# Thirty-two small experts in one stage: second-layer weights held in two column halves, hidden activations streamed

## The reference, cut to what matters

```python
def _L2_ffn_ref(x, router_w, router_b, W1, b1, W2, b2):
    xf = x.reshape(-1, D)                      # D = 64
    logits = xf @ router_w.T + router_b
    idx = jnp.argmax(logits, axis=-1)          # one of 32 experts
    h = jnp.einsum('nd,ndh->nh', xf, jnp.take(W1, idx, axis=0)) + jnp.take(b1, idx, axis=0)
    h = jax.nn.relu(h)                         # 16 hidden units
    out = jnp.einsum('nh,nhd->nd', h, jnp.take(W2, idx, axis=0)) + jnp.take(b2, idx, axis=0)
    return jax.nn.relu(out).reshape(x.shape)
...
h = h + _L2_ffn_ref(_layernorm(h, axis=-1), ...)
```

## Time and profile before

| | us |
|---|---|
| median of 3 runs | 5232.56 |
| lowest and highest | 5227.27, 5240.82 |
| the profiled execution | 5234.82 |
| its span | 5233.0 |
| PE busy | 4141.6 (79%) |
| DVE busy | 2849.0 (54%) |
| ACT busy | 2239.6 (43%) |
| mean granted clock of PE | 0.859 |

### The profile page before, as it was taken

One profiled execution on the slowest core, in us unless ns is written; L12 is line 12 of the kernel. 1 busy time (PEld: TensorE's weight loads), 2 busy tenths in 40 slices (PEclk: granted clock), 3 DMA queues, 4 the chain that ended last, 5 costly groups with the idle time before them and its releaser, 6 DMA issues. The chain is left out here.

```text
span 5233.0 us, 70744 instructions
## 1 busy us (share of the span) xinstructions
PE 4141.6 (79%) x26824; PEld 2791.7 (53%) x26824; DVE 2849.0 (54%) x6188; ACT 2239.6 (43%) x3791; POOL 494.8 (9%) x824
## 2 busy tenths in 40 slices
PE   6785865899887865899887864799887875799887
PEld 4664644565555634465555633555546554555646
DVE  4555746355545746355545747355554747355555
ACT  3342665254241656254242655144432448144432
POOL 0100000201100010201100010111100110111100
PEclk9898976799888986799888886699998986699998
DMA  2000000000000000000000000000000000000000
GB/s 86 3 3 16 1 17 1 0 1 1 1 1 4 1 17 1 0 1 1 1 1 4 1 17 1 0 1 1 1 1 4 1 1 1 1 1 1 1 1 4
DMA packets 28313, 26.52 MB, mean 5 GB/s; under 512 B 10550, under 2 KB 26934, under 8 KB 27450
## 3 DMA queue, kind: packets, MB, share of 16 engines
q1 hardware_dynamic: 27962, 21.98, 1.5%
HBM read 20.40 MB, written 1.57 MB: 4 GB/s over the span
## 5 line engine op out<-in xcount | busy, mean ns | idle before, releaser
L719 ACT ACTIVATE big<-ps,negmax 128x1024 f32<-128x1024 f32 (+1 forms) x672 | 600.1, 899 | 262.3 <-DVE negmax L752 262.2
L752 DVE TENSOR_REDUCE negmax<-ps 128x1 f32<-128x1536 f32 x336 | 590.0, 1758 | 39.3 <-PE ps L622 19.8
L705 ACT COPY big<-ps 128x512 f32<-128x512 f32 x672 | 394.1, 586 | 494.4 <-PE ps L646 491.4
L646 PE MATMUL ps<-cst,big 128*128 128x128 f32 x4032 | 503.3, 275 | 30.3 <-ACT big L719 29.8
L646 PEld LDWEIGHTS ps<-cst,big 128*128 128x128 f32 x4032 | 457.9, 142 | 48.3 <-ACT big L719 39.7
L436 ACT COPY xt<-ps 64x512 f32<-64x512 f32 x144 | 78.5, 580 | 817.5 <-PE ps L428 817.5
L423 PE MATMUL ps<-cst 128*128 128x512 f32 x608 | 319.0, 682 | 127.8 <-DVEq L190 58.2
L615 PE MATMUL ps<-kup,qup 128*128 128x512 f32 (+3 forms) x768 | 357.0, 562 | 41.9 <-POOLq L190 41.1
L408 POOL TENSOR_TENSOR st<-st,cst 128x6 f32<-128x6 f32 x104 | 156.9, 1508 | 2306.9 <-DVE st L396 2302.8
L662 PE MATMUL ps<-big,v 128*32 128x128 f32 (+1 forms) x8064 | 321.9, 277 | 8.1 <-DVE ctxt L1197 6.0
L615 PE MATMUL ps<-klo,qlo 128*128 128x512 f32 (+3 forms) x672 | 313.7, 550 | 2.2
(11 more groups left out here) (397 smaller groups left out, 7451.4 us busy)
## 6 DMA issues: line engine op xcount, KB each, us to landing
rw<-in_w_route SPq DMA_DIRECT2D x128, 64.5 KB, 1.9
cst<-in_consts SPq DMA_DIRECT2D x1, 2671.0 KB, 14.9
cst<-in_consts SPq DMA_DIRECT2D x1, 2670.5 KB, 9.0
big<-in_consts SPq DMA_DIRECT2D x1, 1872.5 KB, 22.2
out_dram<-res SPq DMA_DIRECT2D x4, 384.0 KB, 2.8
experts_in<-in_consts SPq DMA_DIRECT2D x1, 1360.0 KB, 17.7
qup<-in_patches SPq DMA_DIRECT2D x4, 260.0 KB
klo<-in_pe_low SPq DMA_DIRECT2D x2, 384.0 KB, 23.5
```

The lines of the kernel that those rows point to most:

```text
L646: ins = nc.tensor.transpose(turned_bank(kind, u, g)[:, i * P:(i + 1) * P], prob[:, slot_of(kind, u), (4 * g + i) * P:(4 * g + i + 1) * P], ...
L705: copy(pt[:, slot_of(kind, u), g, 0:n], turned_bank(kind, u, g)[:, 0:n]).then_inc(*ph.mark(copier(kind, g)))
L719: nc.scalar.activation(prob[:, slot_of(kind, u), cols], src[:, cols], ACT.Exp, bias=bias, accum_out=part_sum[:, u, k:k + 1]).then_inc(*ph. ...
L752: nc.vector.tensor_reduce(negmax[:, u:u + 1], flat[:, 0:n], AX.X, ALU.max, negate=True)\
```

## The change

The 12 x 5 = 60 products of the second layer become 15 products with 512 moving columns and 12 that join two halves. For each block of 512 tokens (`outputs`), `w2_2` is stationary in four chunks of 128x64, and `hid` moves. Chunks 0 and 2 go into partitions 0 to 63 of a bank, chunks 1 and 3 into partitions 64 to 127; the bias is added into the lower half by a product with K = 32. ACT copies the bank (128x512) to `both_halves`, a part of the buffer `qup` (`add_halves`). Then four products for each block (`added`) hold 128x128 of `both_halves` stationary and move `fold[64]`, into banks 6 and 7, which DVE reads in place of 4 and 5. The first layer's products keep their number and shape, but are written in three blocks with the second layer's between them.

```diff
+                def add_halves(j):
+                    act.wait_ge(*ph.after("halves_psum", j + 1))
+                    nc.scalar.copy(both_halves[:, 512 * j:512 * (j + 1)], ps[:, 4 + j % 2, :]).then_inc(*ph.mark("halves_copied"))
...
+                    if j == NB - 1 and c in (1, 3):
+                        add_halves(c // 2)
+                add_halves(2)
...
-                pe.wait_ge(*ph.after("hid_ready", NB * C2))
-                for t in range(T):
-                    o = ps[:, 4 + t // 6, (t % 6) * D:(t % 6 + 1) * D]
-                        nc.tensor.matmul(o, hid[:, c, t * P:(t + 1) * P], K("w2_2")[:, c * D:(c + 1) * D], start=(c == 0), stop=False)
-                    ins = nc.tensor.matmul(o, xt2[64:96, t * P:(t + 1) * P], K("b2_2")[64:96, :], start=False, stop=True)
...
+                def outputs(j):
+
+                    pe.wait_ge(*ph.after("hid_ready", (j + 1) * C2))
+                    if j > 1:
+                        pe.wait_ge(*ph.after("halves_copied", j - 1))
+                    for c in range(C2):
+                        strip = ps[D * (c % 2):D * (c % 2) + D, 4 + j % 2, :]
+                        nc.tensor.matmul(strip, K("w2_2")[:, c * D:(c + 1) * D], hid[:, c, 512 * j:512 * (j + 1)],
+                                         start=(c < 2), stop=(c == C2 - 1), skip_group_check=True)
+                    nc.tensor.matmul(ps[0:D, 4 + j % 2, :], K("b2_2")[64:96, :], xt2[64:96, 512 * j:512 * (j + 1)],
+                                     start=False, stop=True, skip_group_check=True).then_inc(*ph.mark("halves_psum"))
+
+                def added(j):
+
+                    pe.wait_ge(*ph.after("halves_copied", j + 1))
+                    for t in range(4 * j, 4 * j + 4):
+                        ins = nc.tensor.matmul(ps[:, 6 + t // 6, (t % 6) * D:(t % 6 + 1) * D], both_halves[:, t * P:(t + 1) * P],
+                                               fold[D][:, :], start=True, stop=True)
...
+                hidden(0)
+                hidden(1)
+                outputs(0)
+                hidden(2)
+                outputs(1)
+                added(0)
+                outputs(2)
+                added(1)
+                added(2)
```

More of the change, by code:

```diff
@@ L75 @@
     "moe2": {"rstd_ready": 2, "xt_copied": 6, "hid_ready": 12, "xt_psum": 6, "logit_psum": 1, "hid_psum": 12,
-        "out_psum": 2, "vec_step": 18, "var_ready": 2, "normed": 2},
+        "out_psum": 2, "halves_psum": 3, "halves_copied": 3, "vec_step": 18, "var_ready": 2, "normed": 2},
     "rel3a": {"pool_step": 8, "upper_cleared": 1, "rstd_ready": 4, "rot_used": 6, "xt_copied": 3, "qv_ready": 6,
@@ L286, in build @@
         sparse = work
+        both_halves = qup[:, 1, :]
         qt = qlo[:, 0, :]
@@ L1609, in _ @@
                 transpose_pe(ph, xa, [4, 5, 6], width=P)
[L1610 to L1617, removed]
@@ L1618, in _, with hidden @@
-                pe.wait_ge(*ph.after("hid_ready", NB * C2))
-                for t in range(T):
-                    o = ps[:, 4 + t // 6, (t % 6) * D:(t % 6 + 1) * D]
-                    for c in range(C2):
-                        nc.tensor.matmul(o, hid[:, c, t * P:(t + 1) * P], K("w2_2")[:, c * D:(c + 1) * D], start=(c == 0), stop=False)
-                    ins = nc.tensor.matmul(o, xt2[64:96, t * P:(t + 1) * P], K("b2_2")[64:96, :], start=False, stop=True)
-                    if t % 6 == 5:
-                        ins.then_inc(*ph.mark("out_psum"))
+                def hidden(j):
+                    pe.wait_ge(*ph.after("xt_copied", NB + j + 1))
+                    for c in range(C2):
+                        if j > 0:
+                            pe.wait_ge(*ph.after("hid_ready", (j - 1) * C2 + c + 1))
+                        nc.tensor.matmul(ps[:, c, :], K("w1_2")[:, c * P:(c + 1) * P], xt2[:, 512 * j:512 * (j + 1)],
+                                         start=True, stop=True).then_inc(*ph.mark("hid_psum"))
@@ new lines, in added @@
+                def added(j):
[3 more added lines that the diff above has]
+                                               fold[D][:, :], start=True, stop=True)
+                        if t % 6 == 5:
+                            ins.then_inc(*ph.mark("out_psum"))
+                hidden(0)
@@ L1939, in _ @@
                     dve.wait_ge(*ph.after("out_psum", i + 1))
-                    nc.vector.scalar_tensor_tensor(h[:, 6 * i:6 * i + 6, :], rows_bank([4, 5], i), 0.0, h[:, 6 * i:6 * i + 6, :],
+                    nc.vector.scalar_tensor_tensor(h[:, 6 * i:6 * i + 6, :], rows_bank([6, 7], i), 0.0, h[:, 6 * i:6 * i + 6, :],
                                                    ALU.max, ALU.add)
```

## The result

The changed kernel takes 5183.8 us (median of 4 runs, 5177.4 to 5190.1) where the kernel before took 5236.7 (5227.3 to 5243.5): a ratio of 0.990, 95% interval 0.9878 to 0.9922. That is 52.9 us less; 60 were forecast (5172, range 5155 to 5203). The profiled executions are 5234.8 and 5177.4, 57.4 apart. Run again beside the experiments, it took 5175.7 against 5235.1 (0.9892, 0.9875 to 0.9908): 59.4 us less.

A forecast was written before the change was run, and what follows sets the result against it. PE's time in moe2 was taken as the bound: 11.9 us an image in place of 28.2 saves 65 us, with 5 given back, so 5174.8 profiled and 5172.5 for the median; range 5155 to 5203.

The forecast's parts named there:

- What bounds the stage: In moe2 PE works last, so its time there is on the path one to one; 112.7 us to be replaced.
- The halves pair: New second layer: two column halves run side by side, eight 512-column records in 1.8 us.
- Bias and joining: New second layer: bias 1.2 us a block with shape changes; joinings 2.7 us an image, plus 0.2 for the tail.
- First layer: moe2's 12 first-layer products stay; image 1's first 3.45 us run at the lower level, 12.2 us before and after.
- the 65 us: moe2's second layer: 11.9 us an image at the upper level in place of 28.2, 65 us saved in all.
- Waits: moe2: ACT's copies are covered, at most 0.2 us; without cover about 0.9; the old 0.69 us wait goes.
- The clock in the new layer: moe2's second layer keeps the upper level, being dense; the old had a wide load before each short record.
- Rival 1: The clock falls in moe2's new layer as in the old: 30 us given back, 5203; chance 0.14 whole or in part.
- What is given back in rel3a: Longer PE idle time before L428 can bring the slower pattern, up to 13.6 us either way; 4 us taken.
- Rival 3: Weight loads stay in the open between the new layer's strips: 3.6 us in all, 5176, or 5180; chance 0.06.
- rival 4: Halves don't pair and the clock falls in moe2's new layer: 17 us more, 5250; chance 0.02.

The follow-up runs named there:

- experiment 2: Changed kernel without the two column halves, all four chunks summed in the lower 64 partitions: 5191.5 us, ratio 0.9918 to the kernel before.
- experiment 7: Changed kernel with each block's joining directly behind its own outputs, so PE waits for ACT's copy: 5187.3 us against 5231.8 for the kernel before.
- experiment 3: Kernel before with one 512-column filler product behind each of the 12 tiles of moe2's second layer: 5234.9 us against 5235.1.
- experiment 4: Kernel before with a 512-column filler behind every second tile of moe2's second layer, six an image: 5204.7 us, ratio 0.9937.
- experiment 5: Changed kernel with 24 filler products in place of 15 at the start of rel3a: 5155.5 us, ratio 0.9853 to the kernel before.
- experiment 6: Kernel before with 21 filler products in place of 15 at the start of rel3a: 5223.8 us against 5231.8, ratio 0.9990.
- experiment 9: Changed kernel with 24 rel3a fillers, bias cut into both halves, nine moe2 fillers for four and four new behind the logits: 5145.2 us against 5231.8.
- experiment 10: Changed kernel with 24 rel3a fillers and the bias cut into both halves, moe2's fillers untouched: 5148.8 us against 5235.1, ratio 0.9835.
- experiment 11: Changed kernel with 24 rel3a fillers, cut bias, eight moe2 fillers for four and two new behind the logits: 5138.7 us against 5235.1, ratio 0.9818.

## Why the prediction was right, point by point

- **What bounds the stage.** Right. PE's time in moe2 was on the path one to one: 65.4 us less there. Against the forecast for the profiled execution (5174.8, measured 5177.4) 6 us more were lost behind the stage than the 5 taken (11.0, all in rel3a), and 3.4 were gained in stages that the change doesn't touch. That the two nearly cancel is luck.
- **The halves pair.** Right, and shown by taking the pairing away (experiment 2): 1.87 us for eight records against 3.58. The row of attn2 with 128 columns and that of attn4 with 512 bounded it well.
- **Bias and joining.** The bias was priced at 1.2 us and took 1.0; the joinings with the tail at 2.9 and took 1.03 + 2.00 = 3.0. Second layer and joinings together take 22.28 - 10.65 = 11.6 us at the upper level, 11.9 were given.
- **First layer.** That its slow start "is so before and after" in image 1 was wrong: the level rose with its first product there, and 3.2 to 3.5 us late in images 2 and 4 instead. Over four images it takes 46.2 us, before 45.7, so the sum didn't suffer.
- **What the 65 us are made of**, which the prediction doesn't say. An estimate from the earlier trace rows and these measurements: at the upper level the old layer would take 16.7 us, so of the 28.2 an image 10.8 are the lower level and 0.7 the wait, and the new layer's 11.6 saves another 5.1 by its products. Over four images that is 43 for the clock, 3 for the wait and 20 for the products; experiment 2 puts the pairing at 21.7.
- **Waits.** Right: none in the stage. With the cover gone (experiment 7) a wait costs 0.74 us where 0.9 was given, and in two images of four the level fell as well.
- **The clock in the new layer.** Right. Of the reason given, that in the old layer a wide load stands before each short record, half is shown: dense records among the short ones keep the upper level (experiments 3 and 4). That it is the load and not the shortness is not shown. Rival 1 did not come; its neighbour with three idle gaps an image lost the level in two images, beside idle time.
- **What is given back in rel3a.** The place was right: the level behind PE's idle time, as experiment 5 shows by filling that time. I took 4 us, and it is 11 in the first profile; all four images showed the slow pattern, in both profiles. The end of the range for this (13.6) was nearly reached. With 11 in place of 4 the forecast would have been about 5180, between the two medians measured. The step that failed is the reason given, that a longer idle time brings the slow pattern. The kernel before already spoke against it: its fast images idle 6.17 us, and image 3, a slow one, idles less:

```profile
3386.76 2.77 PE L428 MATMUL ps<-cst,x 128*64 128x128 f32 x12 [5.79 <-DVE st L418]
```

Behind 8.1 us of idle time 18 profiled images are slow and 5 fast (experiments 3 and 4), and behind 5.1 to 6.5 us 6 are slow and 3 fast (the kernel before, experiments 2 and 7). What chooses between the two patterns stays open. Only with the idle time cut to 1.1 us or less (experiments 5, 6, 9, 10 and 11) was L442 or L441 fast in every image.
- **Rival 3**, weight loads in the open: in the changed kernel the loads for 64 columns lie under the running products (1.87 us for four steps of 0.43, 0.15 over; unpaired it is 3.58 for eight steps, 0.14 over, so the 0.15 isn't the price of loads between the halves). The Trainium skill's rule in "TensorE: Matmul & The Clock Gate", Part 3 (The mechanism), that a load overlaps only with a product in another group of rows, is not borne out for two column halves.
- **Slower than before** (rival 4) needed both the pairing and the level to fail. Neither did; without the pairing alone the kernel is still 0.8% faster.

## What to carry to other kernels

Stream the long operand and hold the short one: 64 moving columns behind a load of 128 cost more than the loads themselves when they let PE's clock fall, so read the granted clock of each stretch before you count cycles. When a stage gets shorter, look at the next idle time of PE: what was saved can come back as a lower level behind it, and a run of fillers that ends just before the wait does keeps it (20 us here). Size such fillers by the timeline at both levels: nine and four delayed PE by up to 2.7 us an image behind the logits, eight and two left it waiting 0.3 to 1.1 us for its input and saved 10 us more (96.3 against 86.6).

## What the runs showed of the hardware that I had not expected

- The level can be bought with useless work: twelve extra products of 512 columns an image cost nothing (5234.9 against 5235.1 us), and six made the kernel 24 to 30 us faster.
- Short stretches of idle time, 0.68 us three times in 24 us, went with a fall of the clock inside an otherwise dense stage in two images of four (0.83 and 0.88 in the mean, the slow start of the first layer included). Without them it fell there in no image of the changed kernel.
- A gain in one stage moved the level in another that was not touched: attn4 took 461.3 to 464.8 us in place of 456.6 over four images in the five kernels with long fillers in rel3a. Of the 52 profiled images the 13 in which rel3a to attn3b takes 386.0 us or more all show 112.7 us in attn4, and of the other 39 all but one show 115.5 to 116.3. So where rel3a is slowest, 3 us of it come back in attn4. The cause stays open.
